# A four-layer graph network on one core: drains at the ends of blocks left out, no scatter after the Chebyshev slots, a joint table for x3, and one term's product moved beside the third Chebyshev gather

## The chip, the cores and the metric

The kernel runs on one core of one Trainium2 chip. TensorE (PE) multiplies matrices and also transposes tiles, VectorE (DVE) and ScalarE (ACT) work element by element, GpSimd (POOL) issues the indirect transfers (gathers and scatters by a list of row numbers), and SyncE (SP) issues the plain ones. The metric is the time of one execution in microseconds (us) of the device, as the median over runs.

## The reference, cut to what matters

`x` has N = 100,000 rows (nodes) of C = 96 features; `src` and `dst` name the ends of E = 50,000 edges, sorted by `dst`. Four layers follow one another, each with a residual and a layer norm: ten hops of a weighted propagation (L0), a graph convolution (L1), three Chebyshev filters with an attention over them, a fusing product and a batch norm (L2), and two GINE convolutions (L3). The change is in L2, in the table that L3 reads, and in what ends every phase.

```python
def prop(h):                                    # L2
    return segment_sum(wn[:, None] * h[row], col, num_segments=n)
# _cheb: out = Tx0 @ w[0] + Tx1 @ w[1] + ... + b, with Tx1 = prop(Tx0), Tx2 = 2 * prop(Tx1) - Tx0
feats = [_cheb(x, prop, w2, b2), _cheb(x, prop, w3, b3), _cheb(x, prop, w4, b4)]
scale_w = softmax(concat(feats) @ attn_w + attn_b, axis=1)
h = concat(feats[i] * scale_w[:, i:i+1]) @ fus_w + fus_b
h = batch_norm(h) * bn_gamma + bn_beta          # then relu, residual, layer norm

def _gine_conv(x, src, dst, e, W1, b1, W2, b2): # L3, twice
    agg = segment_sum(relu(x[src] + e), dst)
    return relu(relu((x + agg) @ W1 + b1) @ W2 + b2)
```

## The kernel before

**Nodes and slots.** A node that no edge ends at gets nothing from a propagation. So each layer is computed twice over: once for all nodes as if no edge reached them (the *dense* part, 98 batches of 1024 rows, tag `base` or `conv`), and once for the *slots*, one row per edge position after the sort (EP = 50,176 rows, 49 batches of 1024 rows, tag `ends`). Only the last edge of a run with one `dst` holds that node's true sum (the mask `is_end`). Where a node has edges, its slot row is the right one.

**Phases.** The program is a row of some 36 phases (class `Phase`, L65). Each allots its semaphores, opens a block of code for the five engines, and ends it; at its end the block holds a barrier (L86), then POOL clears the range of the phase's semaphores (L88), then a barrier of all engines follows (L89). Nothing of one phase runs beside another.

**Propagations.** A pass over the edges gathers 392 tiles of 128 rows by an indirect transfer of POOL, in 56 batches of EDGE = 7. There are two forms. `hop_pass` keeps the running sum in one long DVE operation per batch and has PE all but idle. `edge_pass` weighs the rows on ACT (L641), runs the sum in seven small DVE steps (L586) and scales it on ACT (L1871); it takes *jobs* beside it, dense work that ACT, DVE and PE do in between. POOL runs five batches of gathers ahead, and may refill one of its eight raw buffers when ACT has weighed what was in it. The last thing of POOL in a pass is one indirect add (`fix`), for whose landing it waits. The ten hops are `hop_pass` throughout; hops three to eight are a hardware loop of two phases run three times.

**The Chebyshev stage.** `cheb1` and `cheb2` are edge passes with the dense half batches of `ChebRows` as their job; `cheb3` is a `hop_pass` without one. Then `cheb_slots` computes the slots' rows: for each half batch (a *step*, four tiles of 128 rows) and each of the four terms, PE turns four tiles into one PSUM bank (L1538), ACT or DVE copies them to SBUF, and PE multiplies each of the four tiles with the folded weights of power 0 to 3 (L1563). A folded power p covers MIX = 292 columns (three filters of 96, three logits, one pad) from column 96 max(p - 1, 0) on, so 292, 292, 196 and 100 columns. ACT takes each product out of PSUM (L1517), DVE makes the logits' softmax and the weighted sum of the three filters (`mix`, L1466 to L1486), and PE adds the rows' Gram matrix (L1572). The rows go to `mid_slots` by SP, and POOL scatters them over `mid` (L981). From `mid` and `mid_slots`, `cheb_norm` makes `x3` and `x3_slots`; `gine1` gathers from `x3` by `by_dst.other`, the source node of each edge.

```python
2612  hop_pass(nc, k, "cheb3", by_dst, StoreHop(nc, k, cheb_c), cheb_b, k.i_cheb, k.w_cheb, k.f_cheb, k.f_cheb[:, 0:1])
2613  sources = [(0, x2_slots), (1, cheb_a), (2, cheb_b), (3, cheb_c)]
2614  slot_rows(nc, k, "cheb_slots", ChebRows(nc, k, "ends", False, slots, sources, mid_slots, gram=(total, False), turns=2,
2615                                          scatter=(by_dst, mid, k.N - 1), copies=("act", "dve", "act", "dve")))
```

The order within a phase is written out by hand: for each step each engine runs the job's part of that step (`sync`, `vector`, `scalar`, `tensor`), and in an edge pass the job's steps are shared out over the 56 batches behind each batch's own work.

## Time and profile before

| | |
|---|---|
| median of 3 runs | 14892.31 us (14879.5 to 14901.67) |
| profiled execution, its own time | 14902.41 us |
| its span, first to last instruction | 14900.7 us |
| mean granted TensorE clock | 0.614 of full speed |
| busy: DVE, POOL, PE, ACT | 57%, 57%, 34%, 25% of the span |

The stages around the change, by their bounds in the span: the hops 1583 to 7216, `cheb1` 9459 to 10068, `cheb2` to 10678, `cheb3` to 11189, `cheb_slots` to 12064, `cheb_norm` 12070 to 12749, `gine1` to 13286, `gine1_slots` to 13768, `gine2` to 14316, `gine2_slots` to 14901. As phases exclude one another, the kernel's time is the sum of its stages, and a change is to be priced within its own stage. The shares of the whole span say little: DVE's 57% holds two sorts at the start, and POOL's the gathers and scatters of some twenty passes.

### The profile page before, as it was taken

How to read it: one execution, taken by the hardware profiler on the slowest of the kernel's cores; microseconds unless marked ns; L12 is line 12 of the kernel's file. 1: busy time of each engine (PE TensorE's matmuls, PEld its weight loads, DVE VectorE, ACT ScalarE, POOL GpSimd, SP SyncE). 2: the span in 40 equal slices, each digit the busy share in tenths (PEclk: the TensorE clock that was granted, in tenths of full speed). 3: DMA queues.
4: the chain of work that ended last, by engine and by line, in shares of the span. 5: the costliest groups of instructions: out<-in, count | busy, mean ns of one | idle time of the engine just before them, and what ended most of it. 6: DMA issues, size and time to landing. Idle time of an engine off the chain costs nothing. (4 is left out here: it accounts for less than half of the span.)

```text
span 14900.7 us, 104766 instructions
## 1 busy us (share of the span) xinstructions
PE 5032.5 (34%) x25061; PEld 4094.7 (27%) x25061; DVE 8526.5 (57%) x13835; ACT 3799.2 (25%) x9597; POOL 8529.7 (57%) x8672
## 2 busy tenths in 40 slices
PE   0000012000000002100015335576409976888876
PEld 0000002000000001100014334455308866666544
DVE  8860345444444445422577679776644468558765
ACT  0000011000000001100442342466402357654431
POOL 0567777777777777777227630477673410540767
PEclk9855555555555555555555555677659976899555
DMA  6200234433433344311565433344324457777753
GB/s 212 110 5 1 60 96 133 117 111 111 118 111 110 111 119 123 108 54 54 176 210 160 116 102 127 112 136 129 109 78 131 134 200 272 245 243 246 219 166 107
DMA packets 953813, 1967.82 MB, mean 132 GB/s; under 512 B 322912, under 2 KB 330957, under 8 KB 949616
## 3 DMA queue, kind: packets, MB, share of 16 engines
q1 hardware_dynamic: 674928, 1585.65, 31.2%
q0 software_dynamic: 278272, 375.46, 11.2%
q8 instruction: 207, 3.39, 0.1%
q14 instruction: 406, 3.33, 0.1%
HBM read 1192.75 MB, written 783.59 MB: 133 GB/s over the span
## 5 line engine op out<-in xcount | busy, mean ns | idle before, releaser
L724 POOL DMA_INDIRECT hop_odd_raw<-hop_table,i_hop x1176 | 1112.3, 946 | 393.6 <-issue 371.3
L724 POOL DMA_INDIRECT hop_even_raw<-hop_table,i_hop x1176 | 1112.3, 946 | 387.9 <-issue 348.5
L520 POOL DMA_INDIRECT gine_raw<-x,dst_other x392 | 380.4, 970 | 815.1 <-POOLq L89 695.9
L520 POOL DMA_INDIRECT cheb_raw<-x,i_near x392 | 445.7, 1137 | 654.3 <-POOLq L89 535.1
L520 POOL DMA_INDIRECT gine_raw<-conv,i_near x392 | 396.4, 1011 | 611.7 <-POOLq L89 492.4
L1773 POOL DMA_INDIRECT own_raw<-x,i_dst x392 | 388.0, 990 | 602.9 <-POOLq L89 483.7
L981 POOL DMA_INDIRECT mid<-cheb_slots_ends_rows,dst_end x392 | 384.0, 980 | 490.0 <-DVEq L1488 372.9
L1563 PE MATMUL cheb_slots_ends_product<-folded,b_slots_ends_turned_rows 97*128 97x292 f32 (+3 forms) x3136 | 659.6, 353 | 0.0
L1563 PE MATMUL cheb_base_product<-folded,cheb_base_turned_rows 97*128 97x292 f32 x1568 | 565.4, 517 | 180.4 <-ACT cheb_base_mixed L1517 180.4
L748 DVE TENSOR_TENSOR hop_even_rows<-hop_even_raw,hop_even_factors 128x672 f32<-128x672 f32 x168 | 144.9, 862 | 750.1 <-DMA hop_even_raw<-hop_table,i_hop 750.1
L748 DVE TENSOR_TENSOR hop_odd_rows<-hop_odd_raw,hop_odd_factors 128x672 f32<-128x672 f32 x168 | 144.9, 862 | 750.1 <-DMA hop_odd_raw<-hop_table,i_hop 750.1
L1563 PEld LDWEIGHTS cheb_slots_ends_product<-folded,b_slots_ends_turned_rows 96*128 96x128 f32 (+1 forms) x3136 | 545.4, 190 | 90.3
L520 POOL DMA_INDIRECT gcn_raw<-x,dst_other x392 | 382.6, 976 | 248.7 <-ACT gcn_rows L641 125.9
L818 PE MATMUL hop_odd_rows<-hop_odd_chain,src_carries 128*128 128x96 f32 x6 | 2.1, 450 | 1541.0 <-DVE hop_odd_chain L794 1541.0
L520 POOL DMA_INDIRECT cheb_raw<-cheb_table,i_cheb x392 | 448.2, 1143 | 129.4 <-issue 119.2
L818 PE MATMUL hop_even_rows<-hop_even_chain,src_carries 128*128 128x96 f32 x6 | 2.1, 449 | 1535.0 <-DVE hop_even_chain L794 1535.0
L981 POOL DMA_INDIRECT out_dram<-gine_slots_ends_rows,dst_end x392 | 425.5, 1086 | 157.7 <-issue 104.9
L826 ACT ACTIVATE hop_odd_keeps<-src_inner 128x672 f32<-128x672 f32 x168 | 127.7, 762 | 1361.5 <-DVE hop_odd_chain L794 1314.3
L826 ACT ACTIVATE hop_even_keeps<-src_inner 128x672 f32<-128x672 f32 x168 | 127.7, 762 | 1355.6 <-DVE hop_even_chain L794 1309.2
L292 POOL DMA_INDIRECT x_and_map<-sort_dst_entry,src_map_end x392 | 395.2, 1008 | 128.1 <-issue 127.2
L292 POOL DMA_INDIRECT x_and_map<-map_dst_entry,dst_map_end x392 | 381.7, 974 | 128.0 <-issue 127.2
L1985 POOL DMA_INDIRECT hop_sums<-hop_last_sums,src_end x392 | 384.6, 981 | 119.5 <-issue 119.5
(556 smaller groups left out, 22542.2 us busy)
## 6 DMA issues: line engine op xcount, KB each, us to landing
hop_odd_res<-hop_table SPq DMA_DIRECT2D x168, 336.0 KB
hop_table<-hop_odd_sums SPq DMA_DIRECT2D x168, 336.0 KB
hop_even_res<-hop_table SPq DMA_DIRECT2D x168, 336.0 KB
hop_table<-hop_even_sums SPq DMA_DIRECT2D x168, 336.0 KB
start_x_x<-x_and_map SPq DMA_DIRECT2D x98, 400.0 KB, 3.8
x<-start_x_rows SPq DMA_DIRECT2D x98, 400.0 KB
cheb_base_term<-x SPq DMA_DIRECT2D x98, 400.0 KB
mid<-cheb_base_rows SPq DMA_DIRECT2D x98, 400.0 KB
```

Source lines behind the costliest of these rows:

```text
L292: pool.indirect_dma_start(out=self.node_map, out_offset=bass.IndirectOffsetOnAxis(ap=side.map_end[:, t:t + 1], axis=0), in_=self.entry[:, ...
L520: pool.indirect_dma_start(out=raw_rows[:, b % RAW, g, :], out_offset=None, in_=table, in_offset=bass.IndirectOffsetOnAxis(ap=index[:, t:t ...
L724: pool.indirect_dma_start(out=raw_rows[:, b % RAW, g, :], out_offset=None, in_=table, in_offset=bass.IndirectOffsetOnAxis(ap=index[:, t:t ...
L748: nc.vector.tensor_tensor(by_channel(b).rearrange("p c t -> p t c"), raw[:, b % RAW, :, :], spread(weights[:, at], C), ALU.mult).then_inc( ...
L818: nc.tensor.matmul(carried, side.carries[:, :], chain[:, (batches - 1) % LINES, :, EDGE - 1], start=True, stop=True).then_inc(s["carried"], 1)
L826: nc.scalar.activation(keeps[:, b % LINES, :, :], side.inner[:, b * EDGE:(b + 1) * EDGE].unsqueeze(1).to_broadcast([P, C, EDGE]), ACT.Copy ...
L981: pool.indirect_dma_start(out=table, out_offset=bass.IndirectOffsetOnAxis(ap=side.end[:, t:t + 1], axis=0), in_=self.wide_rows[:, m, g, :] ...
L1563: ins = nc.tensor.matmul(into[:, start - self.low:], self.turned_rows[0:rows, q % 2, j, c, :], self.k.folded[0:rows, power, start:MIX], st ...
L1773: pool.indirect_dma_start(out=raw[:, b % RAW, g, :], out_offset=None, in_=table, in_offset=bass.IndirectOffsetOnAxis(ap=index[:, t:t + 1], ...
L1985: pool.indirect_dma_start(out=self.out, out_offset=bass.IndirectOffsetOnAxis(ap=ph.edge["side"].end[:, t:t + 1], axis=0), in_=ph.edge["sum ...
```

## The change

1. `Phase.block` opens its block with `no_gpsimd_drain=True`, and the barrier of all engines at a phase's end is `sem_only`. In the built program POOL has 37 drain instructions where it had 97 in the written-out program: none at the end of a block, none at the barrier, and one for each phase, the one that belongs to the clearing of the semaphore range (L88). Each other engine goes from 65 to 37. The semaphores that gathers and scatters raise are no longer a phase's own: they live through the whole program and count on (class `Arrivals`, `count_gathers`, `count_scatters`).
2. The loop over hops three to eight is written out as six phases.
3. `cheb3` is an edge pass with a job: `ChebRows` with tag `put`, one source (power 0 of `x2_slots`), which stores its product of 292 columns into a new table `part`. DVE copies the turned tiles and takes the products of tiles 1 and 3, ACT those of tiles 0 and 2.
4. `cheb_slots` has three sources, and loads `part`; DVE adds each product from PSUM onto it in place, ACT copies all turned tiles. It scatters nothing.
5. `x3` and `x3_slots` are two parts of one table, and `gine1` gathers from it by `k.i_near`, which names a slot where the source node has edges, and the node otherwise. The count and width of the gathers stay.

```diff
     def block(self):
-        return self.stack.enter_context(self.nc.Block())
+        return self.stack.enter_context(self.nc.Block(no_gpsimd_drain=True))
...
             self.nc.clear_and_free_semaphores(list(self.sems.values()))
-            self.nc.all_engine_barrier()
+            self.nc.all_engine_barrier(sem_only=True)
...
+class Arrivals:
+    def __init__(self, nc, name):
+        self.sem, self.base = nc.alloc_semaphore(name), 0
...
-                        .then_inc(s[f"gathered{b % RAW}"], 16)
+                        .then_inc(k.gathered[b % RAW].sem, 16)
...
         if self.part_out:
+            if 0 <= q < 2 * self.count:
+                m = i % self.DEPTH
+                if q % 2 == 0 and i >= self.DEPTH:
+                    self.left(ph, dve, i - self.DEPTH)
+                for c in (1, 3):
+                    dve.wait_ge(self.sem(ph, "product"), 4 * q + c + 1)
+                    self.nc.vector.tensor_copy(self.mixed[:, m, q % 2 * 4 + c, :], self.product[c][:, 0:MIX])\
+                        .then_inc(self.sem(ph, "moved"), 1)
             return
...
+            for c in range(4):
+                into = self.mixed[:, i % self.DEPTH, q % 2 * 4 + c, :]
+                dve.wait_ge(self.sem(ph, "product"), 4 * q + c + 1)
+                self.nc.vector.tensor_tensor(into, into, self.product[c][:, 0:MIX], ALU.add)\
+                    .then_inc(self.sem(ph, "taken"), 1)
...
-        with nc.Fori(0, (K_HOPS - 4) // 2):
-            hop("hop_odd", StoreHop(nc, k, hop_b, hop_first), hop_a, 0, k.s_hop)
-            hop("hop_even", StoreHop(nc, k, hop_a, hop_first), hop_b, 0, k.s_hop)
+        for n in range((K_HOPS - 4) // 2):
+            hop(f"hop{2 * n + 3}", StoreHop(nc, k, hop_b, hop_first), hop_a, 0, k.s_hop)
+            hop(f"hop{2 * n + 4}", StoreHop(nc, k, hop_a, hop_first), hop_b, 0, k.s_hop)
...
-        hop_pass(nc, k, "cheb3", by_dst, StoreHop(nc, k, cheb_c), cheb_b, k.i_cheb, k.w_cheb, k.f_cheb, k.f_cheb[:, 0:1])
-        sources = [(0, x2_slots), (1, cheb_a), (2, cheb_b), (3, cheb_c)]
-        slot_rows(nc, k, "cheb_slots", ChebRows(nc, k, "ends", False, slots, sources, mid_slots, gram=(total, False), turns=2,
-                                                scatter=(by_dst, mid, k.N - 1), copies=("act", "dve", "act", "dve")))
+        propagate("cheb3", cheb_c, cheb_b, k.i_cheb,
+                  (ChebRows(nc, k, "put", False, slots, [(0, x2_slots)], part, part_out=True, turns=2, copies=("dve",)),))
+        sources = [(1, cheb_a), (2, cheb_b), (3, cheb_c)]
+        slot_rows(nc, k, "cheb_slots", ChebRows(nc, k, "ends", False, slots, sources, mid_slots, part_in=part,
+                                                gram=(total, False), turns=2, side=by_dst, copies=("act", "act", "act")))
```

On PE in `cheb_slots`, one step (of two in a batch) stood like this before: for each of its four tiles one group of transposes for the next step and one product of four terms.

```order
L1538 MATMUL cheb_slots_ends_turned<-ident,cheb_slots_ends_term 96x128 x4
L1563 MATMUL cheb_slots_ends_product<-folded,cheb_slots_ends_turned_rows 128x292 x2
L1563 MATMUL cheb_slots_ends_product<-folded,cheb_slots_ends_turned_rows 128x196
L1563 MATMUL cheb_slots_ends_product<-folded,cheb_slots_ends_turned_rows 128x100
L1538 MATMUL cheb_slots_ends_turned<-ident,cheb_slots_ends_term 96x128 x4
L1563 MATMUL cheb_slots_ends_product<-folded,cheb_slots_ends_turned_rows 128x292 x2
L1563 MATMUL cheb_slots_ends_product<-folded,cheb_slots_ends_turned_rows 128x196
L1563 MATMUL cheb_slots_ends_product<-folded,cheb_slots_ends_turned_rows 128x100
```

Now the last two tiles of the step stand like this, with the Gram product behind them.

```order
L1574 MATMUL cheb_slots_ends_turned<-ident,cheb_slots_ends_term 96x128 x4
L1594 MATMUL cheb_slots_ends_product<-folded,cheb_slots_ends_turned_rows 128x292
L1594 MATMUL cheb_slots_ends_product<-folded,cheb_slots_ends_turned_rows 128x196
L1594 MATMUL cheb_slots_ends_product<-folded,cheb_slots_ends_turned_rows 128x100
L1594 MATMUL cheb_slots_ends_product<-folded,cheb_slots_ends_turned_rows 128x292
L1594 MATMUL cheb_slots_ends_product<-folded,cheb_slots_ends_turned_rows 128x196
L1594 MATMUL cheb_slots_ends_product<-folded,cheb_slots_ends_turned_rows 128x100
L1602 MATMUL cheb_slots_ends_sum<-cheb_slots_ends_rows 96x97 x8
```

One of the two products of 292 columns is gone, and the fourth tile has no group of transposes ahead of it.

On DVE in `cheb_slots` a batch was copies of turned tiles (L1413) around the two halves of the softmax; its rows before, from the first half on:

```order
L1413 COPY cheb_slots_ends_turned_rows<-cheb_slots_ends_turned 96x512 x2
L1447 TENSOR_REDUCE cheb_slots_ends_most<-cheb_slots_ends_mixed 128x8
L1453 TENSOR_TENSOR cheb_slots_ends_score<-cheb_slots_ends_mixed,cheb_slots_ends_most 128x24
L1413 COPY cheb_slots_ends_turned_rows<-cheb_slots_ends_turned 96x512 x2
L1466 TENSOR_REDUCE cheb_slots_ends_most<-cheb_slots_ends_score 128x8
```

Now the four additions from PSUM stand there, and the mix (five operations of 128x768 behind L1508) stands between those of one step and those of the next.

```order
L1457 TENSOR_TENSOR cheb_slots_ends_part<-cheb_slots_ends_part,cheb_slots_ends_product 128x292 x4
L1473 TENSOR_REDUCE cheb_slots_ends_most<-cheb_slots_ends_part 128x8
L1479 TENSOR_TENSOR cheb_slots_ends_score<-cheb_slots_ends_part,cheb_slots_ends_most 128x24
L1457 TENSOR_TENSOR cheb_slots_ends_part<-cheb_slots_ends_part,cheb_slots_ends_product 128x292 x4
L1502 TENSOR_REDUCE cheb_slots_ends_most<-cheb_slots_ends_score 128x8
```

What PE waited for from ACT it now waits for from DVE.

On DVE in `cheb3` one batch of seven gathered tiles was four operations and some of the pass's own.

```order
L748 TENSOR_TENSOR cheb_rows<-cheb_raw,cheb_factors 128x7x96
L785 SCALAR_TENSOR_TENSOR cheb_rows<-cheb_chain,dst_joins,cheb_rows 128x96
L794 SCALAR_TENSOR_TENSOR cheb_chain<-cheb_keeps,cheb_rows 128x672
L767 TENSOR_TENSOR cheb_sums<-cheb_chain,cheb_factors 128x96x7
L748 TENSOR_TENSOR cheb_rows<-cheb_raw,cheb_factors 128x7x96
```

Now a batch is the chain of `edge_pass` and two steps of the job (one step in every fourth batch: 98 steps for 56 batches).

```order
L593 SCALAR_TENSOR_TENSOR cheb_total<-cheb_bridge,dst_joins,cheb_rows 128x96
L593 SCALAR_TENSOR_TENSOR cheb_total<-cheb_total,dst_joins,cheb_rows 128x96 x6
L593 SCALAR_TENSOR_TENSOR cheb_bridge<-cheb_total,dst_joins,cheb_rows 128x96
L1431 COPY cheb_put_turned_rows<-cheb_put_turned 96x512
L1449 COPY cheb_put_mixed<-cheb_put_product 128x292 x2
L1431 COPY cheb_put_turned_rows<-cheb_put_turned 96x512
L1449 COPY cheb_put_mixed<-cheb_put_product 128x292 x2
```

The weighing of the rows has left DVE (it is ACT's in an edge pass), and copies for PE have come.

## Rows read from the trace of the kernel before

**Rows 1.** Windows by stage: cheb3, cheb_slots, gine1, gine2, gine2_slots

```profile
core 0: us, PE busy (x) PEld busy (x) DVE busy (x) ACT busy (x) POOL busy (x), PEclk, DMA share, GB/s
10678.00:11189.00 511.00, 0.71 (x2) 0.50 (x2) 230.34 (x225) 42.47 (x57) 372.41 (x393) 0.50 0.27 76
11189.00:12064.00 875.00, 838.98 (x5488) 747.25 (x5488) 409.26 (x738) 258.41 (x637) 384.01 (x392) 0.98 0.40 129
12749.00:13286.00 537.00, 471.83 (x2746) 352.13 (x2746) 284.43 (x701) 319.88 (x618) 382.02 (x393) 0.89 0.78 253
13768.00:14316.00 548.00, 413.50 (x1374) 280.64 (x1374) 418.99 (x850) 240.45 (x520) 397.98 (x393) 0.54 0.68 212
14316.00:14901.00 585.00, 390.28 (x1372) 276.82 (x1372) 340.69 (x492) 117.56 (x196) 425.53 (x392) 0.58 0.36 123
```

**Rows 2.** Timeline: PE in cheb_slots (start, us, engine, line, out<-in, count)

```profile
11604.87 0.60 PE L1538 MATMUL cheb_slots_ends_turned<-ident,cheb_slots_ends_term 128*96 128x128 f32 x4
11605.31 1.68 PE L1563 MATMUL cheb_slots_ends_product<-folded,b_slots_ends_turned_rows 97*128 97x292 f32 x8
11606.82 1.52 PE L1572 MATMUL cheb_slots_ends_sum<-cheb_slots_ends_rows 128*96 128x97 f32 x16
11608.18 0.60 PE L1538 MATMUL cheb_slots_ends_turned<-ident,cheb_slots_ends_term 128*96 128x128 f32 x4
```

**Rows 3.** Timeline: DVE in cheb_slots, from the mix to the copy behind it

```profile
11623.12 0.16 DVE L1466 TENSOR_REDUCE cheb_slots_ends_most<-cheb_slots_ends_score 128x8 f32<-128x24 f32 x1
...
11627.79 0.96 DVE L1486 TENSOR_TENSOR cheb_slots_ends_rows<-cheb_slots_ends_rows,cheb_slots_ends_weighted 128x768 f32<-128x768 f32 x1
```

**Rows 4.** Groups by line: addition and copy from PSUM, gathers of hops and cheb2

```profile
L1705 DVE TENSOR_TENSOR cheb_norm_x_rows<-cheb_norm_x_product,cheb_norm_x_skip 128x384 f32<-128x384 f32 x196 | 107.2, 547 | 83.6 <-PE cheb_norm_x_product L1143 83.6
L1413 DVE COPY b_slots_ends_turned_rows<-cheb_slots_ends_turned 96x512 f32<-96x512 f32 x196 | 134.7, 687 | 420.1 <-PE cheb_slots_ends_turned L1538 409.7 <-DVE cheb_slots_ends_rows L1486 9.8 <-PE cheb_slots_ends_product L1563 0.6
L724 POOL DMA_INDIRECT hop_odd_raw<-hop_table,i_hop x1176 | 1112.3, 946 | 393.6 <-issue 371.3
L520 POOL DMA_INDIRECT cheb_raw<-cheb_table,i_cheb x392 | 448.2, 1143 | 129.4 <-issue 119.2
```

**Rows 5.** Timeline: ACT and DVE in cheb2, one batch's own work

```profile
10321.50 1.75 ACT L1871 ACTIVATE cheb_sums<-cheb_total,f_cheb 128x96 f32<-128x96 f32 x7
10323.07 2.02 ACT L641 ACTIVATE cheb_rows<-cheb_raw,w_cheb 128x96 f32<-128x96 f32 x7
...
10312.09 2.23 DVE L586 SCALAR_TENSOR_TENSOR cheb_total<-cheb_total,dst_joins,cheb_rows 128x96 f32<-128x96 f32 x6
```

**Rows 6.** Timeline: PE in cheb2, four 292-column products twice

```profile
10314.68 2.13 PE L1563 MATMUL cheb_base_product<-folded,cheb_base_turned_rows 97*128 97x292 f32 x8
...
10320.66 4.26 PE L1563 MATMUL cheb_base_product<-folded,cheb_base_turned_rows 97*128 97x292 f32 x8 [3.41 <-ACT cheb_base_mixed L1517]
```

**Rows 7.** POOL's drains at block ends (count: ns minimum/median/maximum, first and last start)

```profile
L86 POOLq DRAIN  x12: 34/6704/8701, 2086.7 to 7216.5; - x12
L86 POOLq DRAIN  x2: 34/3367/6700, 8926.0 to 8933.7; - x2
L86 POOLq DRAIN  x3: 6700/6704/6704, 10060.1 to 11181.4; - x3
L86 POOLq DRAIN  x1: 8542/8542/8542, 12055.0 to 12055.0; - x1
L86 POOLq DRAIN  x3: 34/6700/6704, 13278.3 to 14308.5; - x3
L86 POOLq DRAIN  x1: 8550/8550/8550, 14891.3 to 14891.3; - x1
```

**Rows 8.** POOL's drains where the semaphores are cleared, whole span

```profile
L88 POOLq DRAIN  x36: 53/99/241, 3.4 to 14900.1; - x36
```

**Rows 9.** Timeline: POOL's first gather of hops three and five (idle before)

```profile
2610.46 0.98 POOL L724 DMA_INDIRECT hop_odd_raw<-hop_table,i_hop  x1 [10.12 <-POOLq L89]
3637.97 0.98 POOL L724 DMA_INDIRECT hop_odd_raw<-hop_table,i_hop  x1 [12.87 <-issue]
```

More of the change, by code:

```diff
@@ L849, in _, with count_gathers @@
             nc.scalar.activation(fix[:, :], carried, ACT.Copy, scale=fix_scale).then_inc(s["fixed"], 1)
+    count_gathers(k, batches)
+def count_gathers(k, batches):
+    for h in range(RAW):
+        k.gathered[h].base += 16 * EDGE * len(range(h, batches, RAW))
 class Rows:
@@ L1344, in __init__ @@
     def __init__(self, nc, k, tag, dense, batches, sources, out, part_in=None, part_out=False, gram=None, turns=1,
-                 scatter=None, copies=("act",)):
+                 side=None, copies=("act",)):
         self.sources = [(f"term{power}", table, power) for power, table in sources]
         self.part_in, self.part_out, self.gram, self.turns, self.copies = part_in, part_out, gram, turns, copies
-        self.low = min(self.from_column(power) for _, _, power in self.sources)
+        self.side = side
         self.narrow = part_in is not None
-        self.signals = ("turned", "taken", "product", "scored", "exponent", "summed") + tuple(
+        self.signals = ("turned", "taken", "moved", "product", "scored", "exponent", "summed") + tuple(
             f"copied{j}" for j in range(len(sources)))
@@ L1357, in __init__ @@
             self.DEPTH = 3
-        super().__init__(nc, k, tag, dense, batches, inputs, out, scatter)
+        super().__init__(nc, k, tag, dense, batches, inputs, out)
     @staticmethod
@@ L1913, in __init__ @@
     def __init__(self, nc, k, out):
-        self.nc, self.table = nc, out
+        self.nc, self.k, self.table = nc, k, out
         self.out = out[0:k.EP, :].rearrange("(p t) c -> p t c", p=P)
@@ L1961 @@
 class ScatterHop(Finish):
-    SEMS = [f"scattered{w}" for w in range(WORK)] + Residual.SEMS
+    SEMS = Residual.SEMS
     def __init__(self, nc, k, out, residual):
@@ L1971, in buffers @@
         self.residual.buffers(ph)
+        self.start = [arrivals.base for arrivals in k.scattered]
     def sync_start(self, ph, sp):
```

125 lines of the change are left out of this document (68 added, 57 removed).

## The prediction

> **What bounds the kernel now.** Phases exclude one another, so I read the windows by stage first and ask of each stage the change touches what its end waits for. `cheb3` takes 511 us, of which POOL is busy 372 with its 392 gathers; PE does nothing and DVE is busy 230 [rows 1]. POOL is the bound: 511/56 is 9.1 us per batch, and the gathers follow one another with 0.95 us of work [rows 4] and about 0.3 between (the 371.3 us of "issue" over 1176 gathers). `cheb_slots` takes 875 us with PE busy 839 at a clock of 0.98: PE is the bound, DVE (409), ACT (258) and POOL (384) have room [rows 1]. `gine1` (537) and `gine2` (548) are what an edge pass with a job costs here [rows 1]. `gine2_slots` is a stage of slots with a low clock: PE busy 390 of 585 us, clock 0.58 [rows 1].
>
> Then I read what POOL does at a block's end. Its drain there lasts 6.70 us after a pass with gathers, 8.7 or 8.5 after one with scatters, and 34 ns in a block without transfers of POOL [rows 7]. It comes after POOL has waited for its last indirect add, so nothing that the next phase needs is late; all engines wait for it. The first gather of a hop comes 10.12 us after POOL's last work [rows 9], and most of that is this drain. The drain of the semaphore range, behind it, takes 53 to 241 ns [rows 8].
>
> **Part 1: `cheb_slots` without power 0.** Before, one tile on PE is a group of transposes (next start 0.44 us later), then four products (1.51 later), so 1.95; the Gram product takes 1.36, from 11606.82 to 11608.18 [rows 2]. A batch of eight tiles is 8 x 1.95 + 1.36 = 17.0 us, and 49 of them 831 of the 866 us ahead of the drain. The products cover 292 + 292 + 196 + 100 = 880 columns in 1.51 us, so a 292-column product is 1.51 x 292/880 = 0.50 us (four of them in 2.13 in `cheb2` [rows 6], 0.53). Without it, and with three groups of transposes for four tiles, a batch is 8 x (1.51 - 0.50) + 6 x 0.44 + 1.36 = 12.1 us: 4.9 us less, 49 times, **-240**.
>
> What may give some back is DVE. It now adds eight products per batch from PSUM; the nearest row is an addition from PSUM of 384 columns, 547 ns [rows 4], so 292 columns take about 0.45. The mix takes 28.75 - 23.12 = 5.6 us [rows 3]. DVE's work is 8 x 0.45 + 5.6 + 0.6 = 9.8 us of 12.1, so it isn't the bound; but while the mix runs it takes no product, and PE has four banks. From the last addition of a step, mix and next addition end 5.6 + 0.45 = 6.05 us later; PE in that time has the Gram product (1.36) and one step (5.4), less the 0.45 by which the addition trails it: it waits about 0 to 0.3 us per batch. I take 0.2, **+10**. If the Gram product fell on the other side it would be 1.1, +54; that is the bound above, 0 the one below. The six copies on ACT (0.6 each) hide under 12.1.
>
> The scatter of the last batch goes: behind the last mix POOL issued eight of them (384/392 = 0.98 us each [rows 1], with the gaps of rows 4 about 1.3) and waited for them to land: about 10 for the issuing and a few more. I take **-12**, between 8 and 17. The first load now carries 1.2 MB of `part` more, at 240 GB/s (253 in `gine1` [rows 1]) 5 us, half of it beside the other loads: **+3**. Per batch SP now moves 3 x 0.39 + 1.2 in and 0.4 out, 2.8 MB in 12.3 us, 225 GB/s, below the 253 of `gine1` [rows 1], so loads stay hidden; if they didn't, 2.8 MB at 253 would be 11.0 us, still below PE. And POOL has no transfer left in this stage, so its 8.54 us [rows 7] go whatever the other drains do: **-8.5**. Sum of part 1: **-247** (bounds -200 to -262).
>
> **Part 2: `cheb3` with a job.** The pass changes from 9.1 us per batch to what the slowest of three engines makes of it. POOL: if its gathers stay at 0.95 us, 8.9 per batch, nothing changes; with 1.01 as in `gine2` (398/393 [rows 1]) they come to 9.2, with 1.14 as in `cheb2` [rows 4] to 10.1. The gathers of `cheb2` run beside DVE's mix of two-input additions; in `cheb3` DVE has only copies and the chain. The Trainium skill (SBUF — State Buffer, "two separate sides") says that a DVE operation with two SBUF inputs holds the port pair it shares with GpSimd exclusively; the longer gathers beside the mix agree with it, and by it those of `cheb3`, without the mix, would not be the 1.14 but nearer 1.0. ACT: scales 1.6 and weighs 1.9 [rows 5], then takes two products per step, at 0.45 as above 4 x 0.45, so 5.3 per batch of two steps: free. DVE: chain 2.23 [rows 5] and 0.6 for its first and last step, two turned copies of 0.69 [rows 4], four products at 0.45, so 6.0: free. But the three hand the work round: ACT's sums and weighing, DVE's chain, the copy, PE's next turn and products, and the takes, with every engine in program order. Half of that chain is PE, which here works in bursts: the same four products take 2.13 us at the high level of its clock and 4.26 at the low one, after it had waited 3.41 [rows 6]. At the high level the round is 1.6 (scale) + 1.3 (two thirds of the weighing, which the chain waits for) + 2.8 (chain) + 0.7 (copy) + 0.44 (turn) + 1.5 (three products) + 0.4 (take), so 8.7 us per batch of two steps: POOL's own pace. At the low one PE's 1.9 doubles: 10.6. The Trainium skill (TensorE: Matmul & The Clock Gate, "HAM oscillation") says that bursts after idle gaps start at the low clock each time; by it the round would be the 10.6.
>
> So the pass lies between 525 (POOL alone with `gine1`'s gathers, 382/393 = 0.97, which is +10, and 4 for the job's start and end: +14) and 583 (42 batches of two steps at 10.6 and 14 of one at POOL's 8.9, 570, and the 13 us that 511 has over 56 x 8.9: +72). I take what passes of this form with a heavier job show, 537 and 548 [rows 1], borders and drain in them as in the 511: upper end of the two, for 1.2 MB of stores per batch more, **+37**.
>
> **Part 3: the drains.** Counted from [rows 7]: between 2086 and 7216 twelve, two of them idle, nine of 6.70 and one of 8.70, 69.0; `gcn` 6.70; `cheb1`, `cheb2`, `cheb3` 20.1; `gine1` and `gine2` 13.4; the last one 8.55. Sum 117.8. (`cheb_slots`' is in part 1. Two more, in `map_dst` and `own`, are worth 4.4 and perhaps 3; left out.) Whether it is saved depends on what the drain waits for. One drain per phase stays, POOL's with the semaphore range. It takes 53 to 241 ns in all 36 phases [rows 8], but always behind a long one. Were it a full drain, it would now be the first and carry the 6.70. For the saving: it is of another kind, and the long one comes after the landing it could wait for. Against: both are drains on the same queue, and nothing in the trace shows one of this kind first. I take it as saved, **-118**, with the other end 0.
>
> **Part 4: small ones.** The loop written out: the first gather of hop five waits 12.87 us behind POOL's last work, that of hop three 10.12 [rows 9]; so the way back costs 2.75, twice, **-5.5**. Against it more code is to be loaded, hidden by 512 us of hop. The lighter barriers, 36 by under 0.1: **-3**. `gine1` from the joint table: the same 392 gathers of 384 bytes, **0**; price if rows of slots lie worse, `gine2`'s 1.01 us for 0.97, +11 of which POOL's 8.9 against 9.6 per batch hides all. `cheb_norm` reads and writes the same: 0.
>
> **Sum.** -247 + 37 - 118 - 5.5 - 3 = -336.5. The profiled execution took 14902.4 (span 14900.7), so 14566; the median of the runs lies 10 lower: **14556 us**, 2.3% faster.
>
> **Rivals.**
> (A) *The wait moves to the drain that stays.* For: it is the first on POOL's queue after the transfers now. Against: its 53 to 241 ns and its own kind. Then part 3 is 0: 14674.
> (B) *`cheb3` is bound by the round of engines, PE at its low level.* For: the 4.26 us row and the clock of 0.54 in `gine2`, and that `put` has only 98 steps of 0.44 + 2.0, 239 us, for PE at the high level. Against: `gine2` itself, at 0.54 and with PE busy 413 us, stays at 548 [rows 1]. It gives +72 for +37: 14591.
> (C) *Slower: PE loses its clock in `cheb_slots`.* If the wait behind each mix let it fall to the low level, a batch would take 24.2 us for 12.1, the stage 593 us more than forecast: 14556 + 593 = 15149. It decides from the point where the loss eats 336 us, that is 6.9 us per batch, more than half of the way to the low level. For: `gine2_slots`, PE busy 67% at 0.58. Against: PE would be busy 12.1 of 12.3 us, more like today's stage (839 of 875, at 0.98) than like `gine2_slots`, where a third is idle [rows 1].
> (D) *The DVE additions bound `cheb_slots`.* If an addition in place from PSUM cost 0.75 instead of 0.45, DVE would have 12.2 us per batch and PE would wait at each mix: +60, 14616.
>
> **How the numbers follow.** The forecast (drains saved, `cheb3` near 548, PE bound) 0.52; (A) 0.26; (B) 0.14; (D) 0.05; (C) 0.02; anything near no change 0.01. Range: the forecast's own bounds are 14520 (all low ends: -15 in part 1, -23 in part 2) to 14600; with (A), 14674, and its own upward ends it reaches to 14695. I give 14515 to 14695. What a measurement tells here from no change is about 0.2%, 30 us. Faster: all cases but (C) and no change, 0.97; same 0.01; slower 0.02.
>
> **What would show it.** `cheb_slots`' window near 615 us with PE busy over 90% at a clock over 0.95, and the mix followed by additions of about 450 ns; PE idle there for DVE's addition over 1 us per batch would prove (D). `cheb3` near 541 us (548 less its drain), gathers of 0.95 to 1.02, PE's clock telling (B). The first gather of a hop about 3.5 us after POOL's last work, where it is 10.1; a drain at the clearing of the semaphores of 6.7 us would prove (A). The rest of the stages unchanged within 1 us each but for these borders; if `gine1` or `cheb_norm` moves by more than 5 us, the joint table did it. The prediction fails above all if the drains' wait is real work of POOL that comes back elsewhere, or if a stage that I hold for unchanged loses its clock.

## The result, and the profile after

The changed kernel takes 14530.42 us (median of 4 runs, 14521.27 to 14534.47) against 14894.22 of the kernel before (4 runs): a ratio of 0.9758, 95% interval 0.9742 to 0.9773. Its profiled execution took 14521.27 us, span 14519.6, against 14902.41 and 14900.7: 381 us between the two spans, where the forecast's sum had 336.

The stages by windows, as in [rows 1] (`cheb3`, `cheb_slots`, `gine1`, `gine2`, `gine2_slots`):

```profile
core 0: us, PE busy (x) PEld busy (x) DVE busy (x) ACT busy (x) POOL busy (x), PEclk, DMA share, GB/s
10562.00:11088.50 526.50, 337.61 (x1178) 242.78 (x1178) 284.08 (x744) 266.92 (x982) 371.73 (x393) 0.77 0.67 223
11088.50:11716.30 627.80, 605.96 (x4312) 559.45 (x4312) 440.88 (x934) 175.38 (x343) 0.00 (x0) 0.98 0.64 219
12400.00:12922.00 522.00, 464.20 (x2746) 347.50 (x2746) 284.44 (x701) 319.55 (x618) 377.81 (x393) 0.91 0.80 260
13403.00:13943.50 540.50, 416.12 (x1374) 282.70 (x1374) 419.30 (x850) 240.34 (x520) 397.33 (x393) 0.54 0.69 215
13943.50:14519.50 576.00, 392.90 (x1372) 278.42 (x1372) 340.68 (x492) 117.49 (x196) 423.87 (x392) 0.59 0.37 124
```

`cheb_slots` is 628 us for 875, still PE's, at 606 busy and a clock of 0.98. `cheb3` is 526.5 for 511, with POOL's gathers as short as they were (371.73/393 = 0.946 us). The drain of the semaphore range, the only one left on POOL, did not take over the wait:

```profile
L88 POOLq DRAIN  x36: 48/80/152, 3.3 to 14519.0; - x36
```

and the first gather of a hop comes 3.13 us behind POOL's last work, where it was 10.12 [rows 9]:

```profile
3089.52 1.62 POOL L1963 DMA_INDIRECT hop_table<-hop_fix,src_fix_row  x1 [10.66 <-issue]
...
3094.27 0.98 POOL L731 DMA_INDIRECT hop_raw<-hop_table,i_hop  x1 [3.13 <-POOLq L89]
```

The table gives each stage's length from one clearing of the semaphores to the next, in the profiled execution of each kernel (the experiments follow below). The stages named neither in it nor below it differ by at most 1.4 us between before and after.

| stage | before | after | block drain back | full barrier | loop unrolled | four terms | scatter back | filled | ACT copies |
|---|---|---|---|---|---|---|---|---|---|
| map_dst | 517.3 | 511.6 | 516.3 | 511.7 | 516.4 | 511.7 | 511.7 | 511.6 | 511.7 |
| hop four | 512.3 | 504.4 | 511.3 | 504.7 | 511.4 | 504.7 | 504.7 | 504.5 | 504.7 |
| hop five | 515.2 | 504.8 | 511.3 | 504.7 | 511.5 | 504.7 | 504.8 | 504.9 | 504.8 |
| hop_last | 1013.9 | 1003.0 | 1011.6 | 1002.9 | 1011.8 | 1002.8 | 1002.8 | 1002.8 | 1002.8 |
| cheb1 | 609.2 | 601.7 | 609.0 | 601.9 | 609.4 | 602.1 | 602.1 | 601.8 | 601.6 |
| cheb3 | 511.4 | 526.8 | 531.5 | 522.9 | 510.5 | 503.6 | 521.1 | 504.6 | 504.4 |
| cheb_slots | 875.4 | 627.9 | 627.9 | 629.0 | 874.1 | 853.2 | 641.9 | 626.4 | 628.4 |
| gine1 | 537.4 | 522.3 | 535.4 | 524.4 | 539.6 | 524.3 | 527.0 | 534.7 | 525.1 |
| gine2_slots | 584.5 | 575.8 | 590.5 | 575.8 | 587.0 | 574.7 | 573.2 | 573.5 | 574.0 |

Of the 381 us, `cheb_slots` gives 247.5 and `gine1` 15.0; `cheb3` takes 15.4 back; the ten hops give 87.2 (5.9 of it the loop's way back), and `map_dst`, `own`, `gcn`, `cheb1`, `cheb2`, `gine2` and `gine2_slots` together 46.3.

PE in `cheb_slots` now, one batch but for its first tile (timeline, columns as in [rows 2]):

```profile
11401.60 1.19 PE L1594 MATMUL cheb_slots_ends_product<-folded,b_slots_ends_turned_rows 96*128 96x292 f32 x6
11402.63 0.60 PE L1574 MATMUL cheb_slots_ends_turned<-ident,cheb_slots_ends_term 128*96 128x128 f32 x4
11403.07 1.19 PE L1594 MATMUL cheb_slots_ends_product<-folded,b_slots_ends_turned_rows 96*128 96x292 f32 x6
11404.09 0.60 PE L1574 MATMUL cheb_slots_ends_turned<-ident,cheb_slots_ends_term 128*96 128x128 f32 x4
11404.53 2.23 PE L1594 MATMUL cheb_slots_ends_product<-folded,b_slots_ends_turned_rows 96*128 96x292 f32 x12
11406.60 1.52 PE L1602 MATMUL cheb_slots_ends_sum<-cheb_slots_ends_rows 128*96 128x97 f32 x16
11407.96 0.60 PE L1574 MATMUL cheb_slots_ends_turned<-ident,cheb_slots_ends_term 128*96 128x128 f32 x4
```

A tile is 0.44 of transposes (11402.63 to 11403.07) and 1.02 of products (to 11404.09), where it was 1.51; the last two tiles of a step have no transposes between them (x12); the Gram product takes 1.36 as before. No row has an idle time before it: PE waits for nobody. From one Gram product to the next it takes 12.22 us here, 17.01 before, and hardly varies through the stage but for its first and last batches.

### The profile page after: what moved, and what is told of

The parts are those of the page before. It is cut to its first block and busy times, and to the rows that moved or that the text cites. A ratio compares the mean times of both kernels' runs of the same rounds, so it can differ in the third digit from the quotient of the medians.

```text
span 14519.6 us, 105608 instructions
## 1 busy us (share of the span) xinstructions
PE 5141.8 (35%) x25061; PEld 4156.3 (29%) x25061; DVE 8613.3 (59%) x14550; ACT 3939.6 (27%) x10228; POOL 8127.0 (56%) x8280
## 5 line engine op out<-in xcount | busy, mean ns | idle before, releaser
L731 POOL DMA_INDIRECT hop_raw<-hop_table,i_hop x2352 | 2219.5, 944 | 734.3 <-issue 686.3
L527 POOL DMA_INDIRECT gine_raw<-x,i_near x392 | 376.2, 960 | 1433.4 <-POOLq L89 1314.2
L755 DVE TENSOR_TENSOR hop_rows<-hop_raw,hop_factors 128x672 f32<-128x672 f32 x336 | 289.8, 863 | 1494.4 <-DMA hop_raw<-hop_table,i_hop 1494.4
L527 POOL DMA_INDIRECT cheb_raw<-cheb_table,i_cheb x784 | 817.0, 1042 | 245.1 <-issue 236.5
L801 DVE TENSOR_TENSOR_SCAN hop_chain<-hop_keeps,hop_rows 128x672 f32<-128x672 f32 x336 | 521.9, 1553 | 11.7
L1594 PE MATMUL cheb_slots_ends_product<-folded,b_slots_ends_turned_rows 96*128 96x292 f32 (+2 forms) x2352 | 452.4, 335 | 0.9 <-DVE cheb_slots_ends_part L1457 0.8
L731 POOL DMA_INDIRECT hop_first_raw<-x_and_map,src_other x392 | 369.9, 944 | 131.6 <-issue 119.2
L731 POOL DMA_INDIRECT hop_last_raw<-hop_table,i_hop x392 | 373.5, 953 | 122.4 <-issue 119.2
L1594 PEld LDWEIGHTS cheb_base_product<-folded,cheb_base_turned_rows 97*128 97x128 f32 x1568 | 353.4, 237 | 302.9 <-ACT cheb_base_mixed L1553 192.8
L731 POOL DMA_INDIRECT hop_second_raw<-hop_table,i_hop x392 | 369.9, 944 | 124.9 <-issue 114.0
```

The costliest lines, as they stand in the source:

```text
L527: pool.indirect_dma_start(out=raw_rows[:, b % RAW, g, :], out_offset=None, in_=table, in_offset=bass.IndirectOffsetOnAxis(ap=index[:, t:t ...
L731: pool.indirect_dma_start(out=raw_rows[:, b % RAW, g, :], out_offset=None, in_=table, in_offset=bass.IndirectOffsetOnAxis(ap=index[:, t:t ...
L755: nc.vector.tensor_tensor(by_channel(b).rearrange("p c t -> p t c"), raw[:, b % RAW, :, :], spread(weights[:, at], C), ALU.mult).then_inc( ...
L801: nc.vector.tensor_tensor_scan(line(chain), line(keeps), rows[b % LINES], 0.0, ALU.mult, ALU.add)\
L1594: ins = nc.tensor.matmul(into[:, start:], self.turned_rows[0:rows, q % 2, j, c, :], self.k.folded[0:rows, power, start:MIX], start=(j == 0 ...
```

## The experiments

**The drains.** One kernel puts the block's drain back, one the full barrier, one puts an ordinary barrier ahead of the clearing.

```diff
-        return self.stack.enter_context(self.nc.Block(no_gpsimd_drain=True))
+        return self.stack.enter_context(self.nc.Block())
```

> The changed kernel, with only the drains at the ends of blocks put back (the barrier of all engines stays the light one). My theory: the long wait belongs to the ordinary drain, and it is paid once in each phase in which POOL issued transfers. Then the stages lengthen by 6.7 to 8.7 us each as they shrank: each hop by 7.9, gcn 6.1, cheb1 to cheb3 7.5 to 8.3, gine1 and gine2 7 to 8, the last 8.7, cheb_slots by nothing (no transfer of POOL there), in all +135 to +145 us over 14530: 14665 to 14675. Rival: the saving in the borders comes from the lighter barrier or from the semaphores that live on; then most of the 7.9 us of a hop stays saved, and the time is below 14600.

It takes 14651.71 us (14643.8 to 14658.94), 121 more than the changed kernel, less than the 135 expected. (The kernel before took 14886.34 beside these runs and 14894.22 beside those of the changed kernel; taken against it, the difference is 129.) Its drains at the ends of blocks, over the whole span:

```profile
L86 POOLq DRAIN  x36: 40/5542/25445, 3.1 to 14648.0; - x36
```

The long ones take 6.70 us after gathers and 8.54 or 8.70 after scatters, as before; the longest is in `own`, whose stage grew by only 2.9 us. The hops are 6.4 to 7.5 us longer (8.6 the last, which ends in scatters), not 7.9: the drains are worth about what their rows said, and one further microsecond per hop has another source. `cheb3` grew by 4.7 us, `gine1` by 13.0 and `gine2_slots` by 14.7, which is not their drains alone; these stages vary between kernels (below).

```diff
-            self.nc.all_engine_barrier(sem_only=True)
+            self.nc.all_engine_barrier()
```

> The changed kernel, with only the full barrier of all engines put back (its drain stands behind the clearing of the semaphores, and blocks end without one). It tells which drain takes the wait. In the changed kernel the drain of the semaphore range is the first one behind the transfers and takes 48 to 152 ns, so it doesn't wait. Theory 1 (the ordinary drain waits, whichever is first): the drain at the barrier, 34 to 40 ns in the kernel before, now takes 6.7 us and the time is again 14665 to 14675. Theory 2 (the wait is one of the block's end alone, or it runs out by itself while the barrier of the block is passed): the drain at the barrier stays under 0.1 us and the time within 5 us of 14530.

14525.98 us (14521.16 to 14536.98), the same as the changed kernel. Both drains on POOL are short:

```profile
L88 POOLq DRAIN  x36: 48/80/116, 3.3 to 14521.6; - x36
L89 POOLq DRAIN  x36: 40/46/117, 3.5 to 14521.9; - x36
```

So theory 2 of this run holds as far as it goes: an ordinary drain at the barrier costs nothing. Whether that is because it is not the block's, or because the drain of the semaphore range and the clearing come first, the next kernel tells.

```diff
+            self.nc.all_engine_barrier()
             self.nc.clear_and_free_semaphores(list(self.sems.values()))
             self.nc.all_engine_barrier(sem_only=True)
```

> The changed kernel with one more barrier of all engines, with its ordinary drains, between the end of the block and the clearing of the semaphores. The drain behind the clearing did not wait (40 to 117 ns), the one at the block's end did (6.7 us). Theory 1 (an ordinary drain waits if it is the first behind the transfers, and the drain of the semaphore range or the clearing had taken that from it): the added drain takes 6.7 us after a pass with gathers, and the time is about 14650 again. Theory 2 (only the drain of the block's end waits, whatever stands first): the added one takes under 0.1 us, and the whole is 3 to 10 us longer than 14530, for 36 barriers.

14673.35 us (2 runs, 14665.2 to 14681.51), 23 above the 14650 of theory 1; 36 further barriers are in it, and no run prices them apart. The wait is back, in the barrier's drain (here L88; the clearing is L89 in this kernel):

```profile
L88 POOLq DRAIN  x36: 40/5542/9201, 3.3 to 14670.5; - x36
L89 POOLq DRAIN  x36: 48/83/268, 3.6 to 14679.3; - x36
```

Theory 1 holds: the first ordinary drain behind POOL's transfers waits, wherever it stands. The drain of the semaphore range doesn't wait when it is the first, and an ordinary one behind it and the clearing doesn't either. What the long drain waits for isn't shown. Nor has any run left the drains out with the gathers' semaphores still a phase's own, and so in the range that is cleared; all that the runs show of the change in the semaphores is that it alone does not take the wait away, since the two variants of the changed kernel with long drains have it.

**The loop.** The kernel before, with the six hops written out.

```diff
-        with nc.Fori(0, (K_HOPS - 4) // 2):
-            hop("hop_odd", StoreHop(nc, k, hop_b, hop_first), hop_a, 0, k.s_hop)
+        for n in range((K_HOPS - 4) // 2):
+            hop(f"hop{2 * n + 3}", StoreHop(nc, k, hop_b, hop_first), hop_a, 0, k.s_hop)
...
```

> The kernel before with the loop over hops three to eight written out as six phases, nothing else. If the way back costs what the idle time of the first gather said (12.87 against 10.12 us, twice), hops five and seven take 512.4 instead of 515.2 and the whole is 5.5 us shorter (14889), which only the stages can show. Rival: code that must be loaded for the written-out hops gives it back, and each of the six is 1 to 3 us longer than 512.4.

14883.57 us against 14886.34 of the kernel before beside it, ratio 0.9999 (0.999 to 1.0009): the total can't tell. The stages do: hops five and seven lose the way back (515.2 to 511.5), and beside that the hops are 0.7 to 1.0 us shorter each, also the two ahead of the loop (0.2 the ninth, 2.0 the last; 9.5 in all). That is the missing microsecond: a gather takes 944 ns on the mean where it took 946, 392 times. The kernel before, then the one with the changed loop, in the group by line:

```profile
L724 POOL DMA_INDIRECT hop_first_raw<-x_and_map,src_other x392 | 370.8, 946 | 135.9 <-issue 119.2 <-POOLq L89 16.7
```

```profile
L724 POOL DMA_INDIRECT hop_first_raw<-x_and_map,src_other x392 | 370.0, 944 | 135.8 <-issue 119.2 <-POOLq L89 16.7
```

It isn't the loop itself: the kernel with the barrier ahead of the clearing has none, and has 946 ns and hops of 512.4 us again. What decides between the two values stays open; as each kernel has one profiled execution, it may be the execution and not the program.

**The moved term and the scatter.** One kernel takes the term back and leaves the scatter out, one does the reverse.

```diff
-        propagate("cheb3", cheb_c, cheb_b, k.i_cheb, (ChebRows(nc, k, "put", ...),))
-        sources = [(1, cheb_a), (2, cheb_b), (3, cheb_c)]
+        hop_pass(nc, k, "cheb3", by_dst, StoreHop(nc, k, cheb_c), cheb_b, k.i_cheb, k.w_cheb, k.f_cheb, k.f_cheb[:, 0:1])
+        sources = [(0, x2_slots), (1, cheb_a), (2, cheb_b), (3, cheb_c)]
...
```

> The changed kernel without the move of the first term: cheb3 is the pass without a job, cheb_slots multiplies all four terms, copies as before, and loads no part; the scatter stays out. It splits the 247.5 us by which cheb_slots shrank. By my sum the product and its transposes are 240, the scatter's tail 12, its drain 8.5, less 10 and 3 for the additions and the load: so cheb_slots takes about 875.4 - 12 - 8.5 = 855 us here, cheb3 504.5, and the whole 14530 + 227 - 22 = 14735. Rival: the scatter also slowed what ran beside it (DVE's mix against POOL's transfers), so that without it cheb_slots with four terms is below 845.

14725.92 us (14722.5 to 14740.28); `cheb_slots` 853.2, `cheb3` 503.6. The scatter with its drain was worth 875.4 - 853.2 = 22.2, the term 853.2 - 627.9 = 225.3. The rival (a scatter that slowed the stage) is not borne out.

```diff
-                                                gram=(total, False), turns=2, side=by_dst, copies=("act", "act", "act")))
+                                                gram=(total, False), turns=2, side=by_dst, copies=("act", "act", "act"),
+                                                scatter=(by_dst, mid, k.N - 1)))
...
```

> The changed kernel, with the scatter of the slots' rows over mid put back into cheb_slots (three terms and part as changed, no drain). 392 scatters of 0.98 us with 0.30 between are 502 us of POOL, less than the 628 of the stage, so if only the tail counts the stage is 10 to 15 us longer: 640, and the whole 14543. Rival: at 12.3 us per batch POOL's 10.2 and the landing of each batch's scatters hold up the row buffers, or DVE's operations with two inputs in SBUF grow beside POOL's: then the stage is 660 or more, and the removed scatter was worth more than its tail.

14537.9 us (14534.99 to 14544.58); `cheb_slots` 641.9, 14.0 more. A scatter is longer than before, 1125 ns on the mean for 980 [rows 1] (384/392), and still hidden; the tail alone counts.

```profile
L996 POOL DMA_INDIRECT mid<-cheb_slots_ends_rows,dst_end x392 | 440.9, 1125 | 201.4 <-issue 158.1 <-DVEq L1524 43.0 <-DMA mid<-cheb_slots_ends_rows,dst_end 0.3
```

**What `cheb3` waits for.** POOL's gathers keep their pace, but its last one, the indirect add that waits for the consumers, comes 32.6 us behind them, where a hop's comes 10.7 (above). In the waits of POOL in `cheb3` (us in total, times, longest):

```profile
POOL cheb_raw L527 <- issue: 117.4, 385, 0.3
POOL hop_table L1963 <- issue: 32.6, 1, 32.6
```

The consumers fall behind by 22 us over the pass: from one batch's chain on DVE to the next it takes 4.8 us with one step of the job and mostly 8.7 to 10.6 with two. The batches of 8.7 have PE at its high level, most of those of 10.6 begin both steps at the low one. The timeline of PE, a slow batch:

```profile
10816.46 1.09 PE L1574 MATMUL cheb_put_turned<-ident,cheb_put_term 128*96 128x128 f32 x4 [3.71 <-DVE cheb_put_turned_rows L1431]
10817.34 4.10 PE L1594 MATMUL cheb_put_product<-folded,cheb_put_turned_rows 97*128 97x292 f32 x8
10821.23 1.06 PE L1574 MATMUL cheb_put_turned<-ident,cheb_put_term 128*96 128x128 f32 x4
10822.08 2.25 PE L1594 MATMUL cheb_put_product<-folded,cheb_put_turned_rows 97*128 97x292 f32 x8
10827.08 0.65 PE L1574 MATMUL cheb_put_turned<-ident,cheb_put_term 128*96 128x128 f32 x4 [2.74 <-DVE cheb_put_turned_rows L1431]
```

PE waits 3.71 us for DVE's copy, starts at its low level (1.2 GHz: 4.10 for four products) and is at the high one (2.4 GHz, 2.25 for four) by the second step's products. The rule of the Trainium skill (TensorE: Matmul & The Clock Gate, "HAM oscillation") that bursts behind long idle gaps start at the low clock agrees with this batch. The next one starts high, at 0.65 us for its turns, behind 2.74 us; yet elsewhere in the pass PE came back low (1.09) behind 2.36 us. The length of the wait alone doesn't decide. Two kernels take one cause away each.

```diff
+                    if getattr(job, "part_out", False):
+                        job.fill(ph)      # five products of 292 columns into a spare bank
...
-                  (ChebRows(nc, k, "put", False, slots, [(0, x2_slots)], part, part_out=True, turns=2, copies=("dve",)),))
+                  (ChebRows(nc, k, "put", False, slots, [(0, x2_slots)], part, part_out=True, turns=1, copies=("dve",)),))
```

> The changed kernel; in cheb3, PE multiplies five times 292 columns more behind each batch's steps, into a spare bank that nothing reads (one bank for the turned tiles instead of two makes room). It fills the 3.7 us in which PE waits for the copy of the turned tile. In the changed kernel the batches of two steps take 8.7 us where PE is at its high level and up to 10.6 where it is at the low one, and the consumers fall 22 us behind the gathers. Theory (the low level of PE costs the 22 us): with PE held at the high level the batches of two steps take 8.7, the pass is bound by POOL, and cheb3 takes 505 to 510 instead of 526.8. Rival (the round of ACT, DVE and PE is the bound at either level, or the bank or the 1.2 MB stores): it stays at 520 or more.

```diff
-                  (ChebRows(nc, k, "put", False, slots, [(0, x2_slots)], part, part_out=True, turns=2, copies=("dve",)),))
+                  (ChebRows(nc, k, "put", False, slots, [(0, x2_slots)], part, part_out=True, turns=2, copies=("act",)),))
```

> The changed kernel; in cheb3 ACT copies the turned tiles in place of DVE. PE waits for that copy for 3.7 us per batch, since on DVE it stands behind the chain of the pass; on ACT it stands behind the weighing alone, 2.8 us earlier, and the chain runs beside PE's products. Theory (the round is the bound): cheb3 takes 505 to 512, POOL's pace, even with PE at its low level. Rival: ACT, with 3.5 + 2 x 0.6 + 4 x 0.41 = 6.3 us of work per batch, waits at the products before it can scale, and the pass stays at 520 or more.

Filled: 14505.51 us (14504.29 to 14505.68). ACT's copies: 14503.93 us (14500.34 to 14513.04), ratio to the kernel before 0.974 (0.9724 to 0.9757). `cheb3` is 504.6 and 504.4 us, a hop's length, and that of `cheb3` without a job (503.6); a further kernel with ACT's copies, below, has 507.2. In the four kernels that have the changed kernel's own `cheb3` and no long drains it is 521.1 to 529.4. The windows of the two, filled first, then ACT's copies (columns as above):

```profile
10565.00:11069.00 504.00, 396.80 (x1736) 297.96 (x1734) 284.87 (x743) 275.08 (x982) 369.73 (x391) 0.93 0.70 233
```

```profile
10565.00:11069.00 504.00, 338.12 (x1178) 229.53 (x1178) 222.80 (x645) 317.72 (x1080) 369.75 (x391) 0.77 0.69 233
```

The first holds the clock at 0.93 and leaves the copies behind DVE's chain; it also has one bank for the turned tiles where the round before had two. The second has the clock of the changed kernel (0.77) and a round without the wait for DVE's chain. Either is enough. So the 22 us are a round in series that PE's low level makes longer than POOL's pace; the 1.2 MB stores, which both kernels have, cost nothing that the stage's length shows.

**Two terms moved.** From here the question was whether more of `cheb_slots` fits under the gathers.

```diff
-                  (ChebRows(nc, k, "put", False, slots, [(0, x2_slots)], part, part_out=True, turns=2, copies=("dve",)),))
-        sources = [(1, cheb_a), (2, cheb_b), (3, cheb_c)]
+                  (ChebRows(nc, k, "put", False, slots, [(0, x2_slots), (1, cheb_a)], part, part_out=True, turns=2, copies=("act", "act")),))
+        sources = [(2, cheb_b), (3, cheb_c)]
...
```

> Two terms moved in place of one: cheb3's job multiplies power 0 and power 1 (of cheb_a, which is finished by then) into part, ACT copies all turned tiles, and cheb_slots has the terms 2 and 3 and adds 196 columns of each product. By the same steps: PE in cheb_slots needs 8 x 0.51 + 4 x 0.44 + 1.36 = 7.2 us per batch, DVE 8 x 0.35 + 5.63 + 0.6 = 9.0, so DVE becomes the bound: 49 x 9.1 + 15 = 465 us for 628. In cheb3 PE has 98 steps of 0.88 + 3.9 = 4.8 us, 470 of POOL's 497: 505 to 530 us. Sum over put_act (14504): -163 + 0 to 25, so 14340 to 14370. Rival: in cheb3 the round of ACT and PE, 9.6 us of PE per batch of two steps with nothing beside the handing over, takes 11 to 12 us, cheb3 is 560 to 600 us and half of the gain is gone: 14400 to 14440.

> As the one before, but DVE copies the turned tiles of power 0 behind the chain of the pass, as the changed kernel does. If the round is what bounds an edge pass with a job, the 2.8 us of the chain and the 0.7 of the copy stand in series with PE's 9.6: 12 to 13 us per batch of two steps, and cheb3 takes 60 to 100 us longer than with ACT's copies. Rival: DVE's copy takes work off ACT (1.2 us per batch) and cheb3 is the same within 10 us.

With ACT's copies 14412.05 us (14406.26 to 14422.07), ratio 0.9683 (0.9667 to 0.9699), the fastest of all; with DVE's for the first term 14464.13 (14463.19 to 14482.0). `cheb3` is 512.6 and 560.7 us: the round again, 48 us for who copies (60 to 100 expected). `cheb_slots` is 526.8, not the 465 of my sum. DVE is busy 359 of 470 us of it and PE 378, neither of them the bound by itself:

```profile
11140.00:11610.00 470.00, 378.23 (x2776) 363.37 (x2775) 358.83 (x851) 105.80 (x217) 0.00 (x0) 0.89 0.67 221
```

```profile
11307.43 1.05 PE L1575 MATMUL cheb_slots_ends_turned<-ident,cheb_slots_ends_term 128*96 128x128 f32 x4 [1.51 <-DMA cheb_slots_ends_part<-part]
...
11318.89 0.80 PE L1595 MATMUL cheb_slots_ends_product<-folded,b_slots_ends_turned_rows 96*128 96x196 f32 x4 [1.71 <-DVE cheb_slots_ends_part L1458]
```

Here PE waits for the load of `part`, there for a bank that DVE has not emptied behind its mix: 35.4 and 28.2 us in the 400 us from 11160. Behind the first of the two waits it works at the low level (1.05 us for four turns, for 0.60), behind the second hardly (0.80 for four products, for 0.69), though the second is the longer. How the 62 us over my sum divide among the load, the banks and the clock isn't shown. The total fell into the rival's interval for another reason than the rival's.

**The joint table.**

```diff
-        edge_pass(nc, k, "gine1", by_dst, Store(nc, k, sums1), x3_all, k.i_near, added=feats,
+        edge_pass(nc, k, "gine1", by_dst, Store(nc, k, sums1), x3, by_dst.other, added=feats,
```

> The changed kernel, but gine1 gathers from the dense part of x3 by the source node, as before; as nothing is scattered, it reads the dense row also where the source node has edges (so that part of the computation is changed). gine1 took 15.0 us less in the changed kernel, 7.9 of which is the border. Theory 1: the other 7.1 us come from the joint table and its index; then gine1 is 529 again and the whole +7. Theory 2: they come from how its work falls into place from run to run (its batches take 6 to 14 us in no fixed rhythm); then it stays between 518 and 526.

> The kernel with ACT's copies in cheb3, with gine1 gathering from the dense part of x3 by the source node (which changes that part of the computation: dense rows also where the source has edges). A second draw for the question of the joint table. gine1 with the joint table and no drain took 522, 524, 524, 527, 525 and 535 us in six kernels, and with the old index 541 in one; in the kernel before, 537 and 540 with a drain of 6.7. Theory 1 (the joint index saves some 8 us): 530 to 541 here. Theory 2 (chance): 520 to 529.

14533.82 us (14523.6 to 14541.69) beside 14530.42, and 14505.45 (14499.6 to 14514.65) beside 14503.93: no difference that the medians can tell. `gine1` is 540.9 and 530.5 us with the old index; with the joint one and without drains it is 522.3, 524.4, 524.3, 527.0, 534.7, 525.1, 525.7 and 530.4. The two groups overlap (534.7 with the joint index, 530.5 with the old one). That the joint index saves a few us is likelier than not and isn't shown; that the stage varies by 12 us from kernel to kernel is.

## Why the prediction was right, point by point

**Part 1, `cheb_slots`.** Forecast -247, measured -247.5. The pieces come close too: the term 240 - 10 - 3 = 227 (225.3), the scatter with its drain 12 + 8.5 = 20.5 (22.2). An addition takes 450 to 460 ns, the estimate 0.45. That the sum fits to half a microsecond is luck: its misses cancel. A batch became 17.01 - 12.22 = 4.79 us shorter, 235 us in 49 batches, where the sum had 240 less the 10 of the coupling. Rival (D) and that coupling of 0.2 us per batch did not occur: PE idles nowhere in the rows above, since the Gram product stands beside the mix. By the prediction's own figures PE has 1.36 + 5.4 - 0.45 = 6.3 us of work for the 6.05 in which DVE takes no product, so 0 was the right reading. Some 10 us of the 235 were lost at the two ends of the stage, where the sum had the 3 of the load. The largest part that the trace shows is PE's wait for the last mixes, with less work beside them; with four terms it is 4.2 us:

```profile
PE cheb_slots_ends_sum L1602 <- DVEq L1524: 8.5, 2, 4.8
```

Rival (C) had no ground: the clock is 0.98.

**Part 2, `cheb3`.** The step was mis-sized: +37 where it is 526.8 - 503.6 = +23 without its border (503.6 is `cheb3` without a job and without drains; by the four kernels with this `cheb3`, +17 to +26). The passes I compared it with have a heavier job. The bounds were built right at the upper end (8.7 and 10.6 us per batch of two steps, both found in the trace) but one assumption was wrong: a batch with one step takes 4.8 us, not POOL's 8.9, because the consumers work off what they are behind. The cause of (B) is shown by the two kernels at 504 us, its size of +72 was too large. The gathers stayed at 0.946, below my 0.97: they stand beside copies and a chain, and the 1.14 us of `cheb2` beside the mix. The 1.14 is a mean of two kinds. In `cheb2` of the changed kernel the gathers that start while the mix's operations of 128x768 run take 1.1 to 1.7 us, all but three of 140; the others, also those that are under way when the mix begins, take 0.94 or little more:

```profile
10002.22 1.61 POOL L527 DMA_INDIRECT cheb_raw<-cheb_table,i_cheb  x1 [0.30 <-issue]
10004.14 1.44 POOL L527 DMA_INDIRECT cheb_raw<-cheb_table,i_cheb  x1 [0.31 <-issue]
10005.88 1.68 POOL L527 DMA_INDIRECT cheb_raw<-cheb_table,i_cheb  x1 [0.30 <-issue]
10007.86 0.94 POOL L527 DMA_INDIRECT cheb_raw<-cheb_table,i_cheb  x1 [0.31 <-issue]
```

DVE's five operations of the mix run from 10002.06 to 10006.74. The rule cited from the Trainium skill (SBUF — State Buffer, "two separate sides") agrees with that, a gather that is under way included. It does not tell why the gathers beside the chain take 0.94 as well, whose small operations (128x96) have two SBUF inputs too.

**Part 3, the drains.** Saved, as forecast: 118 in the sum, 121 us between the medians with and without, 129 when each is taken against the kernel before beside it. With the two that I left out (`map_dst` 4.7, `own` 2.9 in the stages) the sum would have been 125. Rival (A) is wrong for this kernel, but its mechanism exists: the first ordinary drain takes the wait, and only the kind that stays is free of it. The trace before couldn't tell, and 0.26 was a fair price.

**Part 4.** The loop's way back: 5.5 forecast, 5.9 in the stages. The lighter barrier: 3 forecast; with the full one the median is 4 us lower (3 higher when taken against the kernel before beside it), so nothing is shown. `gine1`: 0 forecast, and it took 8 less beyond its drain, open. Not in the sum at all: 2 ns less per gather in the hops, about 0.9 us in most of them, 9.5 in all. `map_dst` shows the 2 ns too (974 to 972 in the kernel with the changed loop), `own` and `gcn` don't (990 to 991, 976 to 977).

**The total.** 14556 forecast, 14530.42 measured, in the range. Between the two profiled executions 381 us went, 44.6 more than the sum's 336.5: `cheb3` (15), the hops' gathers (9.5), `gine1` (8), the two drains left out (7.6), and some 4 in small pieces. Of these, 10 are the 10 that the forecast took off for the median, and 9 are a profiled execution that ran 9 us below the median of its kernel; that leaves the 26. The range's upper end doesn't follow from its own terms: (A) with the upward end of part 1 alone, +47, would reach 14721 and not 14695. Nothing measured came near it.

## What to carry to other kernels

A drain behind software-issued transfers is paid where the first ordinary one stands: count them by stage, and put back each kind alone before you believe that a barrier is dear. Work put beside a stage bound by transfers is free only if the whole round of engines, in their program order, is shorter than the transfers' pace: who makes the small copy that the next engine waits for was worth 22 us with one term and 48 with two, with no operation added or removed. Price a moved product by its columns and its own stage's bound, and look for the next bound (here the load and the emptying of banks) before you move a second one.

## What the runs showed of the hardware that was not expected

POOL's ordinary drain takes 6.7 us behind gathers whose data have landed, even with a barrier passed in between, and 40 to 117 ns once a drain of the semaphore range and the clearing stand ahead of it. An indirect gather of `cheb2` takes 0.94 us, and 1.1 to 1.7 us when it starts while DVE runs operations of 128x768 with two SBUF inputs; one that started before them keeps its 0.94. An indirect gather of the hops takes 944 or 946 ns on the mean, the same in the hops of one profiled execution (953 or 955 in the last); hops are 511.3 or 512.4 us by it. PE, waiting 3.71 us, came back at the low level in most batches of `cheb3`, but behind 2.74 us at the high one; in the kernel with two terms moved it came back low behind 1.51 us.
